# Seven half-size products instead of eight in the second sweep of a graph network, with two pairs of accumulation banks

## The reference

```python
h = relu(layernorm(x))
T1 = adj @ h
T2 = 2 * (adj @ T1) - h
T3 = 2 * (adj @ T2) - T1
x = x + h @ w[0] + T1 @ w[1] + T2 @ w[2] + T3 @ w[3] + bias0
h = relu(layernorm(x))
s = adj @ (tanh(|h|) * h / (|h| + eps))        # |h| is clipped at 10
x = x + (arctanh(|s|) * s / (|s| + eps)) @ kernel + bias1   # |s| is clipped at 0.999
```

## Time and profile before

| what | value |
|---|---|
| median of 3 runs | 1858.72 us (1858.33 to 1859.75) |
| the profiled execution: its own time | 1856.76 us |
| its span | 1854.6 us |
| PE busy | 1799.5 us, 97% |
| DVE busy | 694.2 us, 37% |
| ACT, POOL busy | 149.0 us (8%), 82.0 us (4%) |
| moved by DMA | 663.11 MB, mean 358 GB/s |

### The profile page before, as it was taken

The page is one execution under the profiler, slowest core; times in us unless marked ns, Lnnn a source line. Parts: engine busy times, 40 slices in busy tenths (PEclk is TensorE's granted clock), DMA queues, the critical chain, the costliest instruction groups (busy, mean ns, idle before and its releaser), DMA issues.

```text
span 1854.6 us, 35085 instructions
## 1 busy us (share of the span) xinstructions
PE 1799.5 (97%) x15628; PEld 839.7 (45%) x15628; DVE 694.2 (37%) x1306; ACT 149.0 (8%) x283; POOL 82.0 (4%) x121
## 2 busy tenths in 40 slices
PE   7999999999999999999999999999999999999997
PEld 4544444444444445444444444334444444444444
DVE  7211111111122123000000001568778767776756
ACT  1000000000000000000000000312111101010014
POOL 0000000000000000000000000110000000000003
PEclk9999999999999999999999999999999999999999
DMA  9999999999999986888888785699999999999995
GB/s 370 421 421 421 421 421 415 387 401 386 400 370 379 375 331 228 318 295 300 294 303 302 265 302 205 241 355 398 372 409 393 399 390 401 403 381 412 394 420 202
DMA packets 94884, 663.11 MB, mean 358 GB/s; under 512 B 11408, under 2 KB 13712, under 8 KB 14608
## 3 DMA queue, kind: packets, MB, share of 16 engines
q1 hardware_dynamic: 93744, 660.64, 90.9%
q10 hardware_dynamic: 992, 0.23, 0.1%
HBM read 658.74 MB, written 2.10 MB: 356 GB/s over the span
## 4 chain that ended last, share of the span: by engine, by line
PE 89%; DVE 8%; issue 1%; ACT 0%; ACTq 0%; DVEq 0%
PE row_bank L646 20%; PE work_bank L586 19%; PE row_bank L627 14%; PE row_bank L575 12%; PE work_bank L667 12%; PE work_bank L588 3%; PE row_bank L648 3%; PE work_bank L661 3%; PE turned L743 2%; PE own_bank L685 2%; DVE ring L919 1%; DVE ring L917 1%; DVE ring L922 1%; DVE partial L953 1%; DVE ring L924 0%
## 5 line engine op out<-in xcount | busy, mean ns | idle before, releaser
L588 PE MATMUL work_bank<-ring,nodes 128*64 128x512 f32 x936 | 420.8, 592 | 0.0
L586 PE MATMUL work_bank<-ring,nodes 128*64 128x512 f32 x936 | 420.8, 592 | 0.0
L648 PE MATMUL row_bank<-ring,nodes 128*64 128x512 f32 x968 | 418.4, 592 | 0.0
L646 PE MATMUL row_bank<-ring,nodes 128*64 128x512 f32 x968 | 418.4, 592 | 0.0
L627 PE MATMUL row_bank<-ring 128*32 128x256 f32 x3264 | 286.6, 385 | 0.0
L627 PE MATMUL row_bank<-ring,nodes 128*32 128x256 f32 x2448 | 257.4, 384 | 24.9 <-DVE common L1016 23.3
L667 PE MATMUL work_bank<-ring,nodes 128*32 128x512 f32 x2352 | 274.5, 593 | 7.1 <-DVE nodes L1081 4.6
L575 PE MATMUL row_bank<-ring,nodes 128*64 128x512 f32 x1112 | 269.9, 596 | 6.8 <-DMA ring<-adj_blocks 6.8
L646 PEld LDWEIGHTS row_bank<-ring,nodes 128*64 128x64 f32 x968 | 132.0, 137 | 225.9 <-issue 225.1
L586 PEld LDWEIGHTS work_bank<-ring,nodes 128*64 128x64 f32 x936 | 127.9, 137 | 218.8 <-issue 218.8
L933 DVE TENSOR_TENSOR partial<-partial,work_bank 128x512 f32<-128x512 f32 x102 | 70.2, 688 | 405.0 <-PE work_bank L588 405.0
(11 more groups left out here) (131 smaller groups left out, 891.6 us busy)
## 6 DMA issues: line engine op xcount, KB each, us to landing
ring<-adj_blocks SPq DMA_DIRECT2D x626, 1024.0 KB, 7.9
out<-resid SPq DMA_DIRECT2D x16, 128.0 KB, 1.9
resid<-x SPq DMA_DIRECT2D x7, 256.0 KB, 11.3
resid<-x SPq DMA_DIRECT2D x2, 128.0 KB, 4.3
w_raw<-cheb_weight ACTq DMA_DIRECT2D x2, 64.0 KB, 9.2
bias<-cheb_bias ACTq DMA_DIRECT2D x1, 32.0 KB, 3.2
bias<-hyp_bias ACTq DMA_DIRECT2D x1, 32.0 KB, 5.2
w_raw<-hyp_kernel ACTq DMA_DIRECT2D x2, 16.0 KB, 9.3
```

Source lines behind the costliest of these rows:

```text
L586: nc.tensor.matmul(bank[ODD, :], nodes[:, c * C + k, A, :], data[:, k, :], start=k == 0, stop=k == C - 1)
L588: done = nc.tensor.matmul(bank[EVEN, :], nodes[:, c * C + k, B, :], data[:, k, :], start=k == 0, stop=k == C - 1)
L646: nc.tensor.matmul(bank[ODD, :], nodes[:, c * C + k, A, :], data[:, k, :], start=first and k == 0, stop=last and k == C - 1)
L648: done = nc.tensor.matmul(bank[EVEN, :], nodes[:, c * C + k, B, :], data[:, k, :], start=first and k == 0, stop=last and k == C - 1)
```

## The change

**Where the faster form is used.** Now also in rows 9 to 0 of the second sweep (`FAST_BELOW = 10`): these have 102 `BOTH` visits. In each of the ten rows the third visit (`PLAIN_COLUMN`, column 13) stays plain: for it no mixtures are made. It is written with 32 columns of stationary data, its first 256 columns into the row's `low` bank and its last 256 into a work bank, which `JOIN` adds in with one more instruction. So 92 visits change form.

**Two pairs of banks.** `own_banks` and `row_banks` are used in turn by fast rows, in both sweeps (`pairs`); the `OWN` visits of rows from 6 on go to the three work banks. A fast row's first visit waits for the reading of the row *before the last*.

**Slots given up twice.** Slots 0 to 4 (`GIVEN_UP`) are given up in the second sweep, from the last `AGAIN` of level 3 to the last fast visit, and again in the third sweep as before.

**Three mixing instructions for four.** The first two, independent of each other, are one instruction of twice the size, through a hand-made access pattern (`first_two`).

**Order.** `TURN` of level 2 comes four visits after the row's end (for rows 9 to 0) in place of two; three `AGAIN` visits of level 2 move into rows 1 and 0; bias additions on POOL stand in the list's order; once the first fast visit has come, all matmuls use 32 stationary columns, not 64 (so `TURN` and plain visits have twice the instructions of half the width). The number of loads, 626, is the same.

```diff
-SLOTS, KEPT_SLOTS = 13, 8
-FAST_FROM, LATE_FROM = 6, 8
+SLOTS, GIVEN_UP = 13, 5
+FAST_BELOW, FAST_FROM, LATE_FROM = 10, 6, 8
+PLAIN_COLUMN = NB - 3
...
+        if level == 2 and row < FAST_BELOW:
+            follow(1, ("JOIN", row, 2), lambda: None)
+            visits_to_turn = 4
...
+        if s[0] == "TURN" and s[2] == 2 and s[1] >= LOW:
+            waiting.append(("SUMS", s[1], 3))
...
+    fast = [i for i in in_order if steps[i][0] == "BOTH" and phase_of[i] > 0 and is_fast(steps[i][1], phase_of[i] + 1)]
+
+    plain = [i for i in fast if phase_of[i] == 1 and steps[i][2] == PLAIN_COLUMN]
+    fast = [i for i in fast if i not in plain]
...
+        for level in (3, 4):
+            if last > shared_from[level]:
+                for k in range(GIVEN_UP):
+                    slot_free[k] = max(slot_free[k], shared_to[level])
...
+        pairs = [[own_banks, row_banks][n % 2] for n in range(fast_second)]
+        pairs += [[row_banks, own_banks][n % 2] for n in range(len(fast_rows) - fast_second)]
...
                     elif first:
-                        pe.wait_ge(s_cleared, row)
-                        pe.wait_ge(s_aside, 5 * row)
-                    pe.wait_ge(s_sums, sums_no[c])
+                        pe.wait_ge(s_cleared, row - 1)
+                        pe.wait_ge(s_aside, 5 * (row - 1))
+                    pe.wait_ge(s_sums, sums_no[c, level_read])
...
+                if i in plain:
+                    row = fast_rows.index((r, 2))
+                    low, high = pairs[row]
+                    bank = work_banks[bank_no[i] % 3]
...
+                    for k in range(C):
+                        for columns, to in ((N1, low), (N2, bank)):
+                            for lane in range(0, P, H):
...
                 if kind == "OWN":
-                    bank = own_banks[own_bank[r] % 2]
+                    bank = own_banks[own_bank[r] % 2] if r < FAST_FROM else work_banks[bank_no[i] % 3]
...
-                    nc.vector.tensor_tensor(mix_of(n, 0), block[:, 0:2, N2], block[:, 0:2, N1], ALU.subtract)\
+                    nc.vector.tensor_tensor(first_two(n, block), block[:, :, N2].rearrange("p (k h) n -> p k h n", k=2),
+                                            block[:, 0:2, :].rearrange("p h (k n) -> p k h n", k=2), ALU.subtract)\
                         .then_inc(s_mixed, 1)
-                    nc.vector.tensor_tensor(block[:, 0:2, N2], block[:, 2:4, N2], block[:, 0:2, N2], ALU.subtract)\
-                        .then_inc(s_mixed, 1)
-                    dve.wait_ge(s_mixed, 4 * n + 1)
+                    dve.wait_ge(s_mixed, 3 * n + 1)
                     nc.vector.tensor_tensor(mix_of(n, 1), block[:, 2:4, N2], mix_of(n, 0), ALU.subtract).then_inc(s_mixed, 1)
-                    dve.wait_ge(s_mixed, 4 * n + 3)
+                    dve.wait_ge(s_mixed, 3 * n + 2)
                     nc.vector.tensor_tensor(mix_of(n, 2), block[:, 2:4, N1], mix_of(n, 1), ALU.subtract).then_inc(s_mixed, 1)
```

More of the change, by code:

```diff
@@ L90, in next_is_known @@
         if kind == "AGAIN":
-            summed = ("JOIN", row) if row >= FAST_FROM else ("SUM", row, 3)
+            summed = ("JOIN" if row >= FAST_FROM else "SUM", row, 3)
             return (level[0], col) in known and (level[0] < 4 or summed in steps)
@@ L131, in work_order @@
                 visit(*corner.pop(0))
+            if j == LOW + 2 and r < LOW - 1:
+                for c in reversed(range(r + 1, LOW)):
+                    visit("AGAIN", r, c, 2)
             visit("BOTH", r, j)
@@ L183, in with_sums, with is_fast @@
             waiting.clear()
-    return out
+        if s[0] == "TURN" and s[2] == 2:
+            out.append(("BIAS", s[1]))
+    return out
+def is_fast(row, level):
+    return level == 2 and row < FAST_BELOW or level == 3 and row >= FAST_FROM
 def is_loaded(kind, row, col, level=0):
@@ L294, in chebyshev_hyperbolic_kernel @@
     loads = len(slot_of)
+    spill_at = {bank_no[i]: spill_no[i] for i in spill_no}
+    own_at = {n: s[1] for n, s in enumerate(bank_users) if s[0] == "OWN"}
+    plain_at = {bank_no[i]: fast_rows.index((steps[i][1], 2)) for i in plain}
+    plain_bank = {row: n for n, row in plain_at.items()}
     first_of_row, last_of_row = {}, {}
@@ L346, in chebyshev_hyperbolic_kernel @@
     buffer_turn = {acc_buf[k]: turn_no[k] for k in acc_buf}
-    bias_order = [s[1] for s in steps if s[0] == "TURN" and s[2] == 2]
     known_at, n = {}, 0
@@ L355, in chebyshev_hyperbolic_kernel @@
             known_at[s[1], 4] = n
-    fast_rows = [s[1] for s in steps if s[0] == "SUM" and s[2] == 3 and s[1] >= FAST_FROM]
     norm_at = {s[1]: n + 1 for n, s in enumerate(s for s in steps if s[0] == "NORM")}
@@ new lines, in _ @@
+                    pe.wait_ge(s_landed[slot], landed)
+                    size = F if i < fast[0] else H
+                    for k in range(C):
+                        for part in range(0, F, size):
+                            lane = k % 2 * F + part
+                            done = nc.tensor.matmul(bank[lane:lane + size, :],
+                                                    nodes[:, c * C + k, A if level == 3 else B, part:part + size],
+                                                    data[:, k, :], start=k < 2, stop=k >= 2, tile_position=(0, lane))
@@ L738, in _ @@
                     wide = out_bank[:, :].rearrange("p (c n) -> p c n", c=C)
-                    size = F if level < 3 else H
+                    size = F if i < fast[0] else H
                     for k in range(C):
```

268 lines of the change are left out of this document (168 added, 100 removed).

## The result

| (us) | before | changed |
|---|---|---|
| median of 4 runs beside each other | 1859.24 us (1858.33 to 1861.35) | 1793.35 us (1792.49 to 1795.18) |
| ratio, 95% interval | | 0.9645 [0.9629, 0.9662] |
| the profiled execution, its span | 1856.76, 1854.6 | 1793.74, 1791.8 |
| second sweep | 413.2 | 375.6 |
| passage | 100.5 | 98.2 |

The kernel is faster by 65.9 us; 1791 was forecast, in a range from 1782 to 1816. The profiled spans differ by 62.8 us. Of these the three stages of the earlier trace rows carry 37.6, 2.3 and 23.1, against 37.7, 0 and 30 in the prediction; the rest of the program is 0.2 longer.

A forecast was written before the change was run, and what follows sets the result against it. PE's work was taken to bound the second sweep, PE's waits for L1016 to slow the third: -37.7 + 0 (passage) - 30 = -67.7 us, from 1856.8 to 1789.1 profiled, 1791 us median, range 1782 to 1816.

The forecast's parts named there:

- The second sweep: Second sweep: 92 visits fall from 3.43 to 3.02 us on PE, 0.41 each, -37.7 us; TURN, sums and blocks cost nothing.
- The condition, that DVE keeps up: Second sweep: DVE's mixing stays hidden behind PE, 2.58 beside 3.02 us a visit, 2 us to spare in the worst row.
- Rival E: Second sweep: the form gains nothing, its rounds losing to switching banks or weights; -30 alone, 1829 us; chance 0.02.
- The mixing: DVE's three mixing instructions: 1.25, 0.72 and 0.61 us, together 2.58 us a visit.
- Rival C: Both sweeps: DVE becomes the bound, L1021's step 2.3 us at half rate; +22 and +23, 1904 us; chance 0.05.
- rival D: DVE held up by POOL's column sums, some 3 us each; short rows lose 1 to 2 us; 1795 to 1810; chance 0.11.
- The passage: Stretch between second sweep and fast third-sweep stretch, 100.5 us: change taken as 0, with 12 us as the upper end.
- The upper end of 12 us: Passage: five slots given up, up to five blocks less lie ready, 12.5 us more of transferring at 421 GB/s.
- The third sweep: Fast stretch: L1016 waits (23.3 us) go; PE's floor 498.9, transfers' 505; 537.3 to 507, -30 us, ends -38 and 0.
- Rival B: Transfers hold the third sweep: -12 at 405 GB/s, 1809 us, or 1821 at 396; also the passage's 12 us; chance 0.19.
- The offset of 2.0: Median of the runs taken as 2.0 us above the profiled execution: 1789.1 profiled, 1791 for the median.
- The signs by which the text would be judged: New trace: second sweep about 375 us, L1021 near 1.22, no L1126 wait, clock 1.00, fast stretch 505 to 510, over 415 GB/s.

The follow-up runs named there:

- more_mixes_second: Changed kernel with the last mixing instruction done twice in the second sweep, each waiting for the one before; 1825.23 us, ratio 0.9818 to the kernel before.
- one_pair_third: Changed kernel with the third sweep's fast rows all on one pair of banks again; 1820.92 us, ratio 0.9795 to the kernel before.
- thin_loads: Changed kernel loading three of a block's four chunks from the third sweep's row 4 on, output not the reference's; 1791.01 us, ratio 0.9632 to the kernel before.
- one_pair_second: Changed kernel with the second sweep's fast rows all sharing one pair of banks; 1863.78 us, ratio 1.0032 to the kernel before.

## Why the prediction held, and where a term was off

**The second sweep: as reckoned.** -37.7 forecast, -37.6 measured; 92 visits at 3.02 us, and the same 0.41 for each with 24 of them. `TURN`, sums and blocks cost nothing there, as reckoned. The condition, that DVE keeps up, held with the margin that was worked out, and `more_mixes_second` shows how narrow that is: of 0.72 us more a visit it hides 0.39 and the sweep pays 0.33. Rival E, that the form gains nothing in this sweep, fell with the same numbers.

**The mixing: as reckoned, apart from a little.** DVE's timeline of the changed kernel, second sweep, at two places:

```profile
780.71 1.37 DVE L1021 TENSOR_TENSOR ring<-ring 128x1024 f32<-128x1024 f32 x1
782.12 0.83 DVE L1025 TENSOR_TENSOR ring<-ring 128x512 f32<-128x512 f32 x1
...
783.74 1.48 DVE L1021 TENSOR_TENSOR ring<-ring 128x1024 f32<-128x1024 f32 x1
785.25 1.11 DVE L1025 TENSOR_TENSOR ring<-ring 128x512 f32<-128x512 f32 x1
...
792.56 1.23 DVE L1021 TENSOR_TENSOR ring<-ring 128x1024 f32<-128x1024 f32 x1 [0.35 <-PE own_bank L689]
793.82 0.69 DVE L1025 TENSOR_TENSOR ring<-ring 128x512 f32<-128x512 f32 x1
794.55 0.69 DVE L1027 TENSOR_TENSOR ring<-ring 128x512 f32<-128x512 f32 x1
...
797.57 0.69 DVE L1027 TENSOR_TENSOR ring<-ring 128x512 f32<-128x512 f32 x1
798.18 0.41 DVE L1116 TENSOR_TENSOR common<-common,own_bank 128x256 f32<-128x256 f32 x1
```

The usual case is the second: the steps are 1.26, 0.73 and (798.18 - 797.57) 0.61 us, 2.6 in all beside 3.02 of PE, and DVE then waits for PE. Rival C needed L1021 at 2.3 us; its records are 1.21 to 1.52, so nothing was left of it. The first place is rival D's: POOL makes a column's sums there. Its records in the same stretch, after one from a place where DVE does no mixing:

```profile
748.99 0.46 POOL L585 TENSOR_TENSOR ring<-ring,nodes 128x128 f32<-128x128 f32 x1
...
780.96 1.44 POOL L583 TENSOR_TENSOR ring<-nodes 128x128 f32<-128x128 f32 x1
782.48 0.79 POOL L585 TENSOR_TENSOR ring<-ring,nodes 128x128 f32<-128x128 f32 x1
783.35 0.79 POOL L587 TENSOR_TENSOR ring<-nodes,ring 128x128 f32<-128x128 f32 x1
784.10 1.72 POOL L574 TENSOR_TENSOR resid<-resid,bias 128x256 f32<-128x256 f32 x1
```

Beside them DVE's records grow from 1.23 to 1.48 and from 0.69 to 1.11 us. The Trainium skill (SBUF — State Buffer, "Who interferes with whom") has DVE and POOL take turns at a port pair that they share. The trace agrees: undisturbed, a sum takes POOL 0.46 us, and beside the mixing 0.79 to 1.44, so POOL is held up by up to 1 us in a record, and DVE by at most 0.42, about one undisturbed sum. D's price was too high for this reason: its "whole length, some 3 us" is that of a column's records beside DVE, POOL's own waiting included, where undisturbed the four take under 2 us. The mechanism of D is there, then, but it cost the second sweep nothing, since the 2 us that even the shortest row has to spare cover it.

**The passage: 0 forecast, -2.3 measured**, of which 1.7 is no gain. The visits of half length in the passage, before and after (groups by line and shape, columns as in the earlier trace rows):

```profile
L667 PE MATMUL work_bank<-ring,nodes 128*32 128x512 f32 x352 | 39.9, 593 | 0.3 <-DVE nodes L1081 0.3
```

```profile
L757 PE MATMUL work_bank<-ring,nodes 128*32 128x512 f32 x336 | 38.1, 592 | 0.0
```

16 records fewer are one visit, 1.72 us; the fast stretch has 1620 such records where it had 1604. The visit lies on the other side of the boundary now; it was moved and not saved. The upper end of 12 us for blocks that don't lie ready was not called on; the transfers moved at 299 GB/s there in place of 246, and PE waits for no block.

**The third sweep: the right mechanism, mis-sized.** The step that failed is "I take 507 us, 537.3 - 507 = -30"; it measured 514.2, -23.1, or -24.8 without the visit that was moved in. What was to go went: the waits for L1016 (23.3), and 4.4 us of PE's busy time (509.92 to 507.26, with one visit of 1.72 more in it), most likely the clock's, for which the prediction had the clock's 5.4. Against that stand the moved visit, 1.7, and 2.9 more of idle time in other places (4.1 to 6.9 without L1016's). These four make the 23.1. Two things were wrong in the 507. The transfers were priced at 421 GB/s, the best window, over the whole stretch. The stretch in two parts (columns as in the earlier trace rows):

```profile
1200.40:1240.00 39.60, 39.08 (x600) 22.10 (x596) 32.83 (x54) 7.49 (x13) 4.63 (x5) 1.00 0.96 368
1240.00:1714.60 474.60, 468.19 (x7173) 240.34 (x7169) 373.99 (x569) 57.09 (x96) 38.73 (x40) 1.00 1.01 417
```

Against 421 GB/s the first 40 us lose 5 us and the rest, at 417, some 4.5. And the floors were compared as if the greatest one decides. PE's floor is 498.9 + 1.7 = 500.6 with the visit moved in, and DVE's mixing and the transfers each come so close that each holds the stretch near 512 with the other relieved; together they cost 9 us over the 504.8 without either. How those 9 are shared out between the two, the runs don't show. Rival B, as a pure limit of the transfers at 405 or 396 GB/s, is refuted by `one_pair_third` and `thin_loads`; a part of its cause is in the 514.

**The rest.** The clock is back at 1.00. The offset of 2.0 between the profiled execution and the median didn't come again (1793.74 and 1793.35). That is luck: it hid half of a miss of 4.6 us (1789.1 was the sum for the profiled one). The signs by which the text would be judged came out, 375.6, L1021 at 1.22, no wait for L1126, clock 1.00, but for the stretch: neither within 505 to 510 nor over 415 GB/s.

The Trainium skill's figure of about 358 GB/s (SBUF — State Buffer, "Summary: rules for kernel authors") would forbid the gain in the third sweep. The stretch moved 413 GB/s over 514 us, so the measurement decided against it, as it had before.

## What to carry to other kernels

Here a form that does less arithmetic paid in proportion to the visits, because the helper that prepares it has room in every visit *and* a second set of accumulators lets the next row start while the last is gathered: with one set in the second sweep the same form took 70 us more, all of its gain there and more. Where one price is put on a stretch, use the mean rate of a long stretch and not its best window, and where two floors lie within a few per cent, add something for both: relieving either gave 2 to 3 us of the stretch, both gave 9. And a helper's margin is to be worked out per visit before it is spent: 0.4 us in 3.02 was all there was, and one step of 0.72 us more used it up and cost 31 to 32 us.

## What the runs showed that was not expected

- A gap on PE costs more than its own length. In `one_pair_second` ten gaps of 4.3 to 4.9 us took 48.4 us, and PE was busy for 23.4 us more behind them, at a granted clock of 0.95 in the mean over 447.5 us: nearly half as much again. In `one_pair_third` eight gaps of up to 3.9 us took 23.4 us, and PE was busy for 3.9 more, clock 0.99. Why the one is so much less than the other is open.
- Transfers with a quarter less to bring were busy for almost as long: the share fell only from 1.01 to 0.91 as the rate fell from 413 to 315 GB/s. Why is open.
- A block in the third sweep now takes longer to land, before and after, each from 1240 to 1714:

```profile
DMA to landing us min/median/max: 4.7/8.3/11.5
```

```profile
DMA to landing us min/median/max: 7.3/11.6/15.1
```

  396 GB/s for 8.3 us are 3.3 MB under way, 413 for 11.6 are 4.8. More loads are under way at a time, and PE still hardly waits for one; that they are issued earlier, since slots come free without the gaps, is the likely cause, not a shown one.
- DVE and POOL, side by side, hold each other up unequally: POOL's sums of 0.46 us last up to 1.52, the mixing steps of 0.69 up to 1.11. In the second sweep of the changed kernel this never reached PE, which has no gap there.
